# Building the one-hot tiles of a two-layer graph network with scalar_tensor_tensor in place of tensor_scalar

## The chip, the cores and the metric

The kernel runs on one core of a Trainium2 chip. The metric is the device time of one execution in microseconds. Each core has TensorE (matmuls), VectorE, ScalarE, GpSimd and SyncE, which run their own instruction streams and meet at semaphores, and DMA queues. In the profile they are PE (and PEld, its weight loads), DVE, ACT, POOL and SP.

## The reference

The graph has 12,500 nodes of 128 features and 400,000 edges, sorted by their destination. Two layers follow each other:

```python
h = relu(layernorm(x))
# layer 0
edge_in  = concat([h[src], h[dst], edge_attr])          # 128 + 128 + 64
m        = relu(relu(edge_in @ We1 + be1) @ We2 + be2)   # 32, then 128
node_msg = relu(relu(concat([h[dst], m]) @ Wn1 + bn1) @ Wn2 + bn2)
x = x + h + segment_sum(node_msg, dst)
# layer 1
h = relu(layernorm(x))
H   = einsum('ni,rio->rno', h, W)                        # 8 relations
msg = (H[etype, src] + b[etype]) * weight
x = x + relu(segment_sum(msg, dst))
```

## The kernel before

The edges are padded to 782 chunks of 512, each of them four tiles of 128 edges (TC = 4). As the edges are sorted, the destinations of a chunk mostly lie in a window of W = 32 nodes; should some chunk span more, all is repeated in further passes. Here there is one pass. Three stages of node work (layernorm, projections, transposes, storing tables to memory) surround two loops over the chunks, in which nearly all the time goes.

**Layer 0, per chunk.** GpSimd fetches the source nodes' projected rows with four indirect DMAs, one for each tile (`gather`, L517, into `prow`, which lies in the tensor `shared`). SyncE loads the edge attributes, the destinations spread over 96 partitions (`dst_wide`, in `rows_place`) and the 32 table rows of the window. TensorE sums the first hidden layer from all of these (`sum_h1`: L980, L984, and at last L987, which waits for the gathered rows), and then come three more matmul stages with ScalarE and VectorE between them. VectorE builds two one-hot tensors per chunk in `build_hot`: `hot` (L790, in `match_window`: 128 edges by 4 x 32 window places, f32) and `hotT` (L813: 96 rows by 512 edges, bf16), with which TensorE picks the destination's rows. For each chunk VectorE's order is: the relu of `h1` (L818), `build_hot` of the following chunk (L790, L813), the addition of an older chunk to `agg` (L824), the bias of `msg2` (L828).

**Layer 1, per chunk.** GpSimd gathers the source's 128 features in the same way (L517, into `rows`, in `rows_place`). VectorE builds, in `build_hot1`, for two chunks at a time: the offsets in the window (L878, twice), `hot` again (L790) and four tiny `et_w` (L885, 128 x 8: the edge's weight in its relation's column) for each chunk, the key (L888, relation and place in one number), and then for each chunk a series of four `hot_rel` (L900, 128 x 256: the edge's weight at its key, in `shared`). TensorE multiplies the rows by `hot_rel` (L1080), which sorts them by relation and destination, and `hot` by `et_w` (L1082). ScalarE copies the sums, TensorE projects them with the eight relations' weights (L1093, L1095) and VectorE adds the result (L915).

**Order and buffers.** Everything is written out by hand, with no scheduler: each engine's block has its own loop, pipelined over chunks by `pipelined` (layer 0) and `paired` (layer 1). The gathers have four slots (SL = 4); a slot is free once `sum_h1` (layer 0) or `scatter` (layer 1) of its last chunk has run. `hotT` and `hot_rel` have two buffers, `et_w` and `hot` four. A series of `hot_rel` waits for the `scatter` that used its buffer. What GpSimd runs in the two loops is the gathers and nothing else.

Of the kernel before, what the change touches and what calls it, by code (L numbers as in the profile page):

```python
# [23 lines left out]
def gnn_two_layers(nc, x, src_t, dst_t, etype_t, weight_t, dst_c, edge_cols,  # L24
                   we1, be1, we2, be2, wn1, bn1, wn2, bn2, w_rel, b_rel, out):
    f32, bf16, i32, u32 = mybir.dt.float32, mybir.dt.bfloat16, mybir.dt.int32, mybir.dt.uint32
    ALU, ACT, AX = mybir.AluOpType, mybir.ActivationFunctionType, mybir.AxisListType
    ds = bass.ds

    P = 128  # L30
# [4 lines left out]
    TC = 4  # L35
    CH = TC * P
# [4 lines left out]
    W = 32  # L41
# [4 lines left out]
    R = w_rel.shape[0]  # L46
# [19 lines left out]
    with ctx:  # L66
        def sb(name, shape, dt=f32):
            return ctx.enter_context(nc.sbuf_tensor(name, shape, dt))
# [4 lines left out]
        def slot_sems(name, n=SL):  # L73
            return [sem(f"{name}{k}") for k in range(n)]
# [20 lines left out]
        iota_key = sb("iota_key", [P, R, W])  # L95
        row_i = sb("row_i", [3 * W, 1], i32)
        row_f = sb("row_f", [3 * W, 1])
# [4 lines left out]
        et_key = late[:, 0:NCH * TC]  # L102
        w_f = late[:, NCH * TC:]
# [4 lines left out]
        base_c = sb("base_c", [P, NROW])  # L108
# [44 lines left out]
        dst_wide = [rows_place[0:3 * W, s * CH:(s + 1) * CH].bitcast(i32) for s in range(SL)]  # L153
# [3 lines left out]
        RW = R * W  # L157
        hot_rel = [shared[:, k * TC * RW:(k + 1) * TC * RW].rearrange("p (t n) -> p t n", n=RW) for k in range(2)]
        rel_sums = [h[k].rearrange("p j d -> p (j d)")[:, 0:2 * RW].rearrange("p (r c n) -> p r c n", r=R, c=2) for k in range(2)]
        et_w = [sb(f"et_w{s}", [P, TC, R]) for s in range(SL)]  # L160
        w_sums = [sb(f"w_sums{k}", [R, 2, W]) for k in range(2)]
        offset = [sb(f"offset{k}", [P, 2 * TC]) for k in range(2)]
        key = [sb(f"key{k}", [P, 2 * TC]) for k in range(2)]
# [5 lines left out]
        hotT = [sb(f"hotT{s}", [3 * W, CH], bf16) for s in range(2)]  # L169
# [42 lines left out]
        h1_summed, h2_summed, hot_built = slot_sems("h1_summed"), slot_sems("h2_summed"), slot_sems("hot_built")  # L212
# [131 lines left out]
        def hold(eng):  # L344

            eng.nop(nofuse=True)  # L346
# [337 lines left out]
        def _(dve):  # L684
# [103 lines left out]
            def match_window(c):  # L788

                return dve.scalar_tensor_tensor(  # L790
                    out=hot[c.slot][:, :, :], in0=tiled(iota_f[:, 0:W], TC), scalar=base_c[:, ds(c.i, 1)],
                    in1=wide(dst_f[:, ds(c.i * TC, TC)], W), op0=ALU.add, op1=ALU.is_equal)
# [13 lines left out]
            def build_hot(c):  # L806


                s = c.slot
                match_window(c)  # L810
                dve.wait_ge(dst_wide_landed[s], 16 * c.turn + 16)
                hold(dve)
                dve.tensor_scalar(hotT[s % 2][:, :], dst_wide[s], base_c[0:3 * W, ds(c.i, 1)], row_f[:, 0:1],  # L813
                                  ALU.subtract, ALU.is_equal).then_inc(hot_built[s], 1)

            def relu_h1(c):
                dve.wait_ge(h1_summed[c.slot], c.turn + 2)
# [12 lines left out]
            def step(c, before, before2, after):  # L830
                if c:
                    relu_h1(c)
                if after:
                    build_hot(after)
                if before2:
                    add_chunk(before2)
                if before:
                    bias_msg2(before)

            with dve.Fori(0, passes) as m:  # L840
                dve.wait_ge(pass_ready, m + 1)
                hold(dve)
                build_hot(Chunk(m, 0, 0))
                pipelined(m, dve, step)

                set_windows(m + 1, pass_step, pass_ready, 2 * m + 2)
# [25 lines left out]
            def build_hot1(p):  # L872


                k = p.half
                for n, c in enumerate(p.chunks):

                    dve.tensor_scalar(offset[k][:, n * TC:(n + 1) * TC], dst_f[:, ds(c.i * TC, TC)], base_c[:, ds(c.i, 1)],  # L878
                                      -1.0, ALU.subtract, ALU.max).then_inc(offsets_set, 1)
                for n, c in enumerate(p.chunks):  # L880
                    dve.wait_ge(scattered[c.slot], c.turn + 1)
                    match_window(c)
                    for t in range(TC):
                        at = ds(c.i * TC + t, 1)
                        dve.tensor_scalar(et_w[c.slot][:, t, :], iota_key[:, :, 0], et_key[:, at], w_f[:, at],  # L885
                                          ALU.is_equal, ALU.mult)
                dve.wait_ge(offsets_set, 2 * p.n + 2)
                dve.scalar_tensor_tensor(out=key[k][:, :], in0=offset[k][:, :], scalar=float(W), in1=et_key[:, p.tiles],  # L888
                                         op0=ALU.min, op1=ALU.add).then_inc(keys_set, 1)
                dve.wait_ge(keys_set, p.n + 1)  # L890
                for n, c in enumerate(p.chunks):
                    u = c.slot

                    if p.half:
                        dve.wait_ge(scattered[u - 2], p.m * SLOT_USES[u - 2] + p.quad + 2)
                    else:
                        dve.wait_ge(scattered[u + 2], p.m * SLOT_USES[u + 2] + p.quad + 1)
                        dve.wait_ge(scattered[u], c.turn + 1)
                    for t in range(TC):
                        ins = dve.tensor_scalar(hot_rel[u % 2][:, t, :], iota_key[:, :, :].rearrange("p r n -> p (r n)"),  # L900
                                                key[k][:, n * TC + t:n * TC + t + 1], w_f[:, ds(c.i * TC + t, 1)],
                                                ALU.is_equal, ALU.mult)
                    ins.then_inc(hot1_built[u], 1)

            def add_pair(p):
# [12 lines left out]
            def step1(pair, before, after):  # L918
                if after:
                    build_hot1(after)  # L920
                if before:
                    add_pair(before)

            with dve.Fori(0, passes) as m:
                set_windows(m, pass1_step, pass1_ready, 2 * m)
                dve.wait_ge(pass1_ready, m + 1)
                hold(dve)
                build_hot1(Pair(m, 0, 0))
                paired(m, dve, step1)


            for g in range(NG):
                for a, (t0, t1) in enumerate(HALVES):
# [3 lines left out]
                                             op0=ALU.max, op1=ALU.add).then_inc(fin_done, 1)  # L937
# [236 lines left out]
```

## Time and profile before

| | |
|---|---|
| median of 3 runs | 8168.06 us (8164.82 to 8168.57) |
| the profiled execution's own time | 8177.98 us |
| its span, first to last instruction | 8176.1 us |
| mean granted TensorE clock | 0.939 |
| busy: PE, PEld | 6794.7 us (83%), 5258.3 us (64%) |
| busy: POOL, DVE, ACT | 6070.7 (74%), 3968.1 (49%), 2015.0 us (25%) |
| gathers of layer 0 | from 94.9 us on, the last starts at 4140.6 us |
| gathers of layer 1 | from 4212.4 us on, the last starts at 8136.4 us |

In this profile a row of the grouped view has the line, the engine, the operation, what is written and read, the shapes and the count; behind the bar the busy time in us and the mean of one in ns, and behind the second bar the idle time of the engine in front of these instructions with what ended it. "issue" means that the profile shows nothing the engine waited for. A row of the view in time order has the start in us, the length in us, the engine, the line and the count of merged instructions; the engine's idle time before it stands in brackets. The names `shared`, `rows_place` and `late` are large tensors that hold several buffers each: `shared<-p_tab,idx` is layer 0's gather, `rows_place<-h_tab,idx` is layer 1's, and `shared<-iota_key,key,late` is `hot_rel`.

### The profile page before, as it was taken

The numbers are of one execution on the slowest core, as the hardware profiler recorded it, in microseconds if no ns is written. First come the engines' busy times: TensorE is split into PE (matmuls) and PEld (weight loads), VectorE is DVE, ScalarE is ACT, GpSimd is POOL, SyncE is SP. The second block draws the span as 40 slices with busy tenths as digits, with TensorE's granted clock in tenths as the row PEclk, the third lists the DMA queues.
The fourth block names the chain that finished last, engine by engine and source line by source line (L and its number), as shares of the span: only waits on it lengthen the run. The fifth ranks groups of instructions, "written<-read, shape, count | busy, mean of one in ns | idle before, by whom it ended". The sixth has DMA issues, their size and how long they took to land.

```text
span 8176.1 us, 180555 instructions
## 1 busy us (share of the span) xinstructions
PE 6794.7 (83%) x52954; PEld 5258.3 (64%) x52954; DVE 3968.1 (49%) x13460; ACT 2015.0 (25%) x4976; POOL 6070.7 (74%) x6300
## 2 busy tenths in 40 slices
PE   5999999999988999999967787777777777877777
PEld 4666666666666666666656666666666666666665
DVE  5333333333333333333355555555555555555555
ACT  5333333333333333333330000000000000000000
POOL 4777777777777777777757777777777777777776
PEclk7999999999999999999988888988898888888889
DMA  6333333333333333333332222222222222222222
GB/s 130 83 81 81 81 80 80 81 81 81 81 80 81 81 81 81 81 81 80 81 85 53 53 53 53 53 52 53 53 53 53 53 53 53 53 53 53 52 53 75
DMA packets 627942, 566.94 MB, mean 69 GB/s; under 512 B 312595, under 2 KB 502171, under 8 KB 627420
## 3 DMA queue, kind: packets, MB, share of 16 engines
q0 software_dynamic: 200192, 256.65, 15.5%
q1 hardware_dynamic: 427724, 309.99, 13.3%
q8 instruction: 10, 0.16, 0.0%
q14 instruction: 16, 0.13, 0.0%
HBM read 544.42 MB, written 21.68 MB: 69 GB/s over the span
## 4 chain that ended last, share of the span: by engine, by line
POOL 35%; PE 29%; issue 26%; DMA 7%; DVE 1%; ACT 1%; POOLq 1%; SPq 0%; DVEq 0%; ACTq 0%
POOL shared L517 31%; PE bank L1080 19%; DMA rows_place<-h_tab,idx 6%; PE bank L1093 5%; POOL rows_place L517 4%; PE bank L1082 3%; PE bank L1095 1%; ACT h_place L560 1%; PE bank L994 0%; PE bank L1013 0%; POOLq L346 0%; POOLq L512 0%; DMA qr_tab<-late 0%; DVE stats L690 0%; SPq L411 0%
## 5 line engine op out<-in xcount | busy, mean ns | idle before, releaser
L517 POOL DMA_INDIRECT shared<-p_tab,idx x3128 | 3056.4, 977 | 997.1 <-issue 957.4
L517 POOL DMA_INDIRECT rows_place<-h_tab,idx x3128 | 2970.6, 950 | 978.1 <-issue 847.7
L1080 PE MATMUL bank<-shared,rows_place 128*128 128x256 f32 x6256 | 1830.8, 443 | 876.6 <-issue 756.7
L1080 PEld LDWEIGHTS bank<-shared,rows_place 128*128 128x128 f32 x6256 | 1290.7, 217 | 1140.4 <-issue 791.5
L900 DVE TENSOR_SCALAR shared<-iota_key,key,late 128x256 f32<-128x256 f32 x3128 | 1130.9, 423 | 740.6 <-PE bank L1082 603.5
L669 ACT ACTIVATE h_place<-bank 128x256 f32<-128x256 f32 x782 | 300.6, 384 | 3581.6 <-PE bank L1082 3102.2
L994 PE MATMUL bank<-h_sb,w_tile 128*128 128x128 f32 x6256 | 907.6, 288 | 69.5 <-DVE h_sb L818 0.9
L994 PEld LDWEIGHTS bank<-h_sb,w_tile 128*128 128x128 f32 x6256 | 758.5, 191 | 279.6 <-DVE h_sb L818 279.6
L818 DVE TENSOR_SCALAR h_sb<-bank,be_col 128x128 f32<-128x128 f32 x782 | 274.1, 351 | 1339.1 <-PE bank L987 1339.1
L1013 PE MATMUL bank<-wn_half,h_sb 128*128 128x128 f32 x6256 | 890.3, 285 | 0.0
L1093 PE MATMUL bank<-h_place,w_rel_sb 128*128 128x64 f32 x6256 | 859.8, 295 | 0.0
L1093 PEld LDWEIGHTS bank<-h_place,w_rel_sb 128*128 128x128 f32 x6256 | 804.2, 208 | 26.6
L828 DVE TENSOR_TENSOR shared<-bank,bn_rep 128x512 f32<-128x512 f32 x782 | 540.9, 692 | 539.9 <-PE bank L1013 539.9
L1013 PEld LDWEIGHTS bank<-wn_half,h_sb 128*128 128x128 f32 x6256 | 762.3, 192 | 0.0
L620 ACT ACTIVATE shared<-bank,be_col 128x512 f32<-128x512 f32 x782 | 537.4, 687 | 750.7 <-PE bank L994 750.7
L624 ACT ACTIVATE shared<-shared 128x512 f32<-128x512 f32 x782 | 493.2, 631 | 904.3 <-DVE shared L828 822.4
L885 DVE TENSOR_SCALAR et_w<-iota_key,late 128x8 f32<-128x8 f32 x3128 | 694.7, 300 | 0.0
L987 PE MATMUL bank<-ident,shared 128*128 128x128 f32 x1564 | 382.5, 326 | 314.6 <-DMA shared<-p_tab,idx 313.8
L980 PE MATMUL bank<-shared,w_pair 128*128 128x128 f32 x3128 | 557.6, 301 | 51.3 <-DMA shared<-in_edge_cols 51.3
L980 PEld LDWEIGHTS bank<-shared,w_pair 128*128 128x128 f32 x3128 | 408.4, 190 | 291.4 <-issue 240.0
L915 DVE TENSOR_TENSOR agg<-agg,bank 128x32 f32 x782 | 147.6, 189 | 815.3 <-PE bank L1095 498.4
L790 DVE SCALAR_TENSOR_TENSOR hot<-iota_f,base_c,dst_f 128x128 f32<-128x128 f32 x1564 | 536.1, 343 | 1.2 <-issue 1.2
(93 smaller groups left out, 5328.6 us busy)
## 6 DMA issues: line engine op xcount, KB each, us to landing
rows_place<-in_dst_c SPq DMA_DIRECT2D x782, 192.0 KB
shared<-in_edge_cols SPq DMA_DIRECT2D x782, 128.0 KB
shared<-p_tab,idx POOLq DMA_INDIRECT x3128
rows_place<-h_tab,idx POOLq DMA_INDIRECT x3128
qr_w<-qr_tab SPq DMA_DIRECT2D x782, 18.0 KB
qr_tab<-late SPq DMA_DIRECT2D x21, 336.0 KB, 5.7
res<-in_x SPq DMA_DIRECT2D x14, 448.0 KB, 6.9
idx<-in_src_t SPq DMA_DIRECT2D x392, 8.0 KB
```

The source lines that it names most:

```text
L517: pool.indirect_dma_start(out=rows_of[s][:, t, :], out_offset=None, in_=table, in_offset=bass.IndirectOffsetOnAxis(ap=idx[k][:, s * TC + t ...
L620: act.activation(msg1_sb[:, :], ps_msg1[:, :], ACT.Relu, bias=be2_col[:, 0:1]).then_inc(msg1_done, 1)
L624: act.activation(msg2_sb[:, :], msg2_sb[:, :], ACT.Relu).then_inc(msg2_done, 1)
L790: return dve.scalar_tensor_tensor(out=hot[c.slot][:, :, :], in0=tiled(iota_f[:, 0:W], TC), scalar=base_c[:, ds(c.i, 1)], in1=wide(dst_f[:, ...
L828: dve.tensor_tensor(msg2_sb[:, :], ps_msg2[:, :], bn2_rep[:, :], ALU.add).then_inc(msg2_biased, 1)
L885: dve.tensor_scalar(et_w[c.slot][:, t, :], iota_key[:, :, 0], et_key[:, at], w_f[:, at], ALU.is_equal, ALU.mult)
L900: ins = dve.tensor_scalar(hot_rel[u % 2][:, t, :], iota_key[:, :, :].rearrange("p r n -> p (r n)"), key[k][:, n * TC + t:n * TC + t + 1], ...
L980: pe.matmul(ps_h1[:, 0:P], w1_pair[:, q, :], ea[s][:, q * P:(q + 1) * P], start=(q == 0), stop=False)
L994: ins = pe.matmul(ps_msg1[:, t * P:(t + 1) * P], w2_tile[:, t, :], h1_sb[:, :], start=True, stop=True)
L1013: ins = pe.matmul(ps_msg2[:, t * P:(t + 1) * P], h2_sb[:, b * P:(b + 1) * P], wn2_half[:, a, :], start=True, stop=True)
L1080: pe.matmul(bank[s][:, 0:RW], rows[s][:, t, :], hot_rel[s % 2][:, t, :], start=(t == 0), stop=(t == TC - 1))
L1093: pe.matmul(there, w_rel_sb[:, r, :], rel_sums[p.half][:, r, :, :].rearrange("p c n -> p (c n)"), start=(r == 0), stop=False)
```

## The change

Three instructions are written with another operation. `tensor_scalar` takes one tensor and two scalars, here both a column with one value for each partition, and does two operations with them. `scalar_tensor_tensor` takes a tensor, one scalar and a second tensor. The second column becomes this second tensor, by repeating it along the row (`broadcast_to`, no copy in memory). The computed values, the shapes, the types and the waits are the same, and so is the order of the instructions on each engine: on VectorE 782 `hotT`, 3128 `et_w` and 3128 `hot_rel` are SCALAR_TENSOR_TENSOR in place of TENSOR_SCALAR, and on the other engines nothing differs.

```diff
@@ build_hot (layer 0) @@
                 dve.wait_ge(dst_wide_landed[s], 16 * c.turn + 16)
                 hold(dve)
-                dve.tensor_scalar(hotT[s % 2][:, :], dst_wide[s], base_c[0:3 * W, ds(c.i, 1)], row_f[:, 0:1],
-                                  ALU.subtract, ALU.is_equal).then_inc(hot_built[s], 1)
+                dve.scalar_tensor_tensor(out=hotT[s % 2][:, :], in0=dst_wide[s], scalar=base_c[0:3 * W, ds(c.i, 1)],
+                                         in1=row_f[:, 0:1].broadcast_to([3 * W, CH]), op0=ALU.subtract, op1=ALU.is_equal)\
+                   .then_inc(hot_built[s], 1)
@@ build_hot1 (layer 1) @@
                     for t in range(TC):
                         at = ds(c.i * TC + t, 1)
-                        dve.tensor_scalar(et_w[c.slot][:, t, :], iota_key[:, :, 0], et_key[:, at], w_f[:, at],
-                                          ALU.is_equal, ALU.mult)
+                        dve.scalar_tensor_tensor(out=et_w[c.slot][:, t, :], in0=iota_key[:, :, 0], scalar=et_key[:, at],
+                                                 in1=w_f[:, at].broadcast_to([P, R]), op0=ALU.is_equal, op1=ALU.mult)
...
                     for t in range(TC):
-                        ins = dve.tensor_scalar(hot_rel[u % 2][:, t, :], iota_key[:, :, :].rearrange("p r n -> p (r n)"),
-                                                key[k][:, n * TC + t:n * TC + t + 1], w_f[:, ds(c.i * TC + t, 1)],
-                                                ALU.is_equal, ALU.mult)
+                        ins = dve.scalar_tensor_tensor(
+                            out=hot_rel[u % 2][:, t, :], in0=iota_key[:, :, :].rearrange("p r n -> p (r n)"),
+                            scalar=key[k][:, n * TC + t:n * TC + t + 1],
+                            in1=w_f[:, ds(c.i * TC + t, 1)].broadcast_to([P, RW]), op0=ALU.is_equal, op1=ALU.mult)
                     ins.then_inc(hot1_built[u], 1)
```

## Rows read from the trace of the kernel before

**Rows 1.** The page's busy totals: busy us (share of the span) and instructions.
```profile
PE 6794.7 (83%) x52954; PEld 5258.3 (64%) x52954; DVE 3968.1 (49%) x13460; ACT 2015.0 (25%) x4976; POOL 6070.7 (74%) x6300
```

**Rows 2.** The page's costliest groups: the gathers, hot_rel and the bias of msg2.
```profile
L517 POOL DMA_INDIRECT shared<-p_tab,idx x3128 | 3056.4, 977 | 997.1 <-issue 957.4
L517 POOL DMA_INDIRECT rows_place<-h_tab,idx x3128 | 2970.6, 950 | 978.1 <-issue 847.7
L900 DVE TENSOR_SCALAR shared<-iota_key,key,late 128x256 f32<-128x256 f32 x3128 | 1130.9, 423 | 740.6 <-PE bank L1082 603.5
...
L828 DVE TENSOR_TENSOR shared<-bank,bn_rep 128x512 f32<-128x512 f32 x782 | 540.9, 692 | 539.9 <-PE bank L1013 539.9
```

**Rows 3.** The view of L517: duration ns min/median/max, first and last start us.
```profile
L517 POOL DMA_INDIRECT shared<-p_tab,idx x3128: 940/945/1218, 94.9 to 4140.6; - x196
L517 POOL DMA_INDIRECT rows_place<-h_tab,idx x3128: 940/945/1133, 4212.4 to 8136.4; - x196
```

**Rows 4.** Waits: us in total, times, longest us.
```profile
PE bank L987 <- DMA shared<-p_tab,idx: 313.8, 752, 1.6
...
POOL shared L517 <- DMA idx<-in_src_t: 37.3, 1, 37.3
```

**Rows 5.** In order of time, layer 0, one chunk: VectorE and GpSimd.
```profile
1999.52 0.54 DVE L813 TENSOR_SCALAR hotT<-rows_place,base_c,row_f 96x512 bf16<-96x512 int32 x1
...
1999.80 1.07 POOL L517 DMA_INDIRECT shared<-p_tab,idx  x1 [0.30 <-issue]
...
2000.83 0.19 DVE L824 TENSOR_TENSOR agg<-agg,bank 128x32 f32 x1 [0.78 <-PE bank L1029]
2001.18 0.94 POOL L517 DMA_INDIRECT shared<-p_tab,idx  x1 [0.30 <-issue]
...
2002.43 0.95 POOL L517 DMA_INDIRECT shared<-p_tab,idx  x1 [0.30 <-issue]
...
2003.68 0.94 POOL L517 DMA_INDIRECT shared<-p_tab,idx  x1 [0.31 <-issue]
...
2004.60 0.54 DVE L813 TENSOR_SCALAR hotT<-rows_place,base_c,row_f 96x512 bf16<-96x512 int32 x1
...
2004.93 1.03 POOL L517 DMA_INDIRECT shared<-p_tab,idx  x1 [0.30 <-issue]
```

**Rows 6.** In order of time, layer 0: three meetings of hotT and a gather.
```profile
2158.82 0.57 DVE L813 TENSOR_SCALAR hotT<-rows_place,base_c,row_f 96x512 bf16<-96x512 int32 x1
2158.93 0.94 POOL L517 DMA_INDIRECT shared<-p_tab,idx  x1 [0.30 <-issue]
...
2565.23 0.54 DVE L813 TENSOR_SCALAR hotT<-rows_place,base_c,row_f 96x512 bf16<-96x512 int32 x1
2565.36 1.22 POOL L517 DMA_INDIRECT shared<-p_tab,idx  x1 [0.30 <-issue]
...
2862.27 0.54 DVE L813 TENSOR_SCALAR hotT<-rows_place,base_c,row_f 96x512 bf16<-96x512 int32 x1
2862.69 0.94 POOL L517 DMA_INDIRECT shared<-p_tab,idx  x1 [0.30 <-issue]
```

**Rows 7.** In order of time, layer 1: hot (L790) and a gather, twice.
```profile
4543.45 0.34 DVE L790 SCALAR_TENSOR_TENSOR hot<-iota_f,base_c,dst_f 128x128 f32<-128x128 f32 x1
4543.54 1.07 POOL L517 DMA_INDIRECT rows_place<-h_tab,idx  x1 [0.30 <-PE bank L1082]
...
7513.15 0.34 DVE L790 SCALAR_TENSOR_TENSOR hot<-iota_f,base_c,dst_f 128x128 f32<-128x128 f32 x1
7513.17 1.13 POOL L517 DMA_INDIRECT rows_place<-h_tab,idx  x1 [0.30 <-PE bank L1082]
```

**Rows 8.** Views of single lines, VectorE: duration ns min/median/max, first and last start.
```profile
L813 DVE TENSOR_SCALAR hotT<-rows_place,base_c,row_f x782: 533/536/712, 142.6 to 4139.8; 96x512 bf16<-96x512 int32 x196
L900 DVE TENSOR_SCALAR shared<-iota_key,key,late x3128: 394/406/653, 4214.7 to 8132.1; 128x256 f32<-128x256 f32 x196
L885 DVE TENSOR_SCALAR et_w<-iota_key,late x3128: 274/283/547, 4212.5 to 8128.5; 128x8 f32<-128x8 f32 x196
L790 DVE SCALAR_TENSOR_TENSOR hot<-iota_f,base_c,dst_f x1564: 335/343/353, 135.3 to 8127.7; 128x128 f32<-128x128 f32 x196
L888 DVE SCALAR_TENSOR_TENSOR key<-offset,late x391: 149/156/233, 4214.4 to 8128.7; 128x8 f32<-128x8 f32 x196
```

**Rows 9.** In order of time, layer 1: a series of hot_rel and a gather.
```profile
4254.99 1.38 DVE L900 TENSOR_SCALAR shared<-iota_key,key,late 128x256 f32<-128x256 f32 x4 [0.22 <-DVE key L888]
...
4255.46 1.08 POOL L517 DMA_INDIRECT rows_place<-h_tab,idx  x1 [0.30 <-issue]
```

## The prediction

> **What bounds the kernel now.** Read first the busy totals [rows 1]: TensorE is busy for 83% of the span, GpSimd for 74%, VectorE for 49%. That looks like a kernel bound by TensorE, but the GpSimd share leaves out the short pause before each gather. In the costliest groups [rows 2] the 3128 gathers of layer 0 take 3056.4 us, with 997.1 us of idle time before them, together 4053.5 us; by their first and last start and their length [rows 3] they stand from 94.9 to 4141.5 us, 4046.6 us. So no time in layer 0 is without a gather or its pause (one wait of 37.3 us, for the indices, comes early on [rows 4]). The same sum in layer 1 is 2970.6 + 978.1 = 3948.7 us, against 4212.4 to 8137.3 us = 3925 us (the first idle stretch lies before it). The median gather is 0.945 us and the pause 0.30 [rows 3, 5]: GpSimd starts one every 1.249 us and never waits for a slot. TensorE waits for it instead: in 752 of 782 chunks of layer 0 the matmul of L987 waits for the gathered rows [rows 4]. Whatever lengthens a gather lengthens the kernel by as much, and what VectorE takes longer for costs nothing by itself.
>
> What lengthens gathers now? The mean of layer 0 is 977 ns against a usual 0.944 us: 3128 x 33 ns = 103 us in all, 132 ns per chunk of four. Layer 1 has 950 ns: 3128 x 6 = 18 us. In time order [rows 5] three gathers of four take 0.94 or 0.95 us, and the fourth, which starts while hotT (L813) runs, takes 1.03 to 1.07. The extra time follows a formula. In [rows 6] hotT starts at 2565.23 and ends at 2565.77; the gather started at 2565.36 and took 1.22, 0.28 too much. The end of hotT less 0.28 is 2565.49, 0.13 us after the gather's start. At 2004.60 + 0.54 = 2005.14 and a gather from 2004.93 with 0.09 extra it is 0.12. So a gather wants something 0.125 us after its start that hotT holds to its end. Two edges confirm it: where hotT ends at 2862.81 and the gather started at 2862.69, it is not held up; where hotT starts at 2158.82 and the gather at 2158.93, the moment (2159.06) falls 0.24 us after hotT's start, the gather gets through at 0.94 and hotT takes 0.57 in place of 0.54. At 0.26 us after the start (the 2565 case) hotT was ahead. A two-scalar TENSOR_SCALAR holds that something from about 0.25 us after its start to its end.
>
> **Does a SCALAR_TENSOR_TENSOR hold it?** This decides the case. The trace has one with two SBUF inputs and a column as scalar: hot, L790. In layer 0 it is over before the gather's moment, but in layer 1 it meets it 22 times, and each of the 22 gathers is held up. In [rows 7] L790 runs from 4543.45 to 4543.79, the gather from 4543.54 takes 1.07, 0.13 too much: 4543.66, 0.12 after the start, as before. At 7513.15 it starts 0.02 before the gather and still holds it up by 0.19. So it holds from at most 0.15 us after its start: a wider share of the instruction than now. Its second input is a broadcast column too (dst_f, repeated along each window).
>
> A rule of the Trainium skill speaks against me in part. Its page "SBUF — State Buffer", section "Who interferes with whom", says that a VectorE instruction with two SBUF inputs contends only with a GpSimd instruction that reads SBUF, and infers that such an operation does not stall a software DMA, whose descriptors need the write interface. By the inference the change would free the gathers, and the sum would be the rival "freed" below. The L790 rows contradict it for this indirect gather.
>
> **The change part by part.** No instruction moves, and no wait or DMA is added; three kinds of instruction get other durations and another hold.
>
> hotT, 782 times in layer 0. Now 536 ns for 512 elements [rows 8]. L900 takes 406 for 256 and L885 283 for 8: 123 ns for 248 elements, about 0.5 ns each, so TENSOR_SCALAR from SBUF moves two elements per 1.04 ns. SCALAR_TENSOR_TENSOR has two rows: L888 with 8 elements 156 ns (no column scalar), L790 with 128 elements and a column 343. I take 1.04 ns per element, as L828 bears out (512 elements from PSUM, 692 [rows 2]), and 343 - 133 = 210 ns fixed: 210 + 533 = 743 ns, 207 more than now. Ends: 692 as L828, and 275 (L885's fixed part) + 533 = 808. The phase of hotT to the gather stays: L987 waits for a gather, L818, L790 and L813 follow at fixed distances, and the held gather is the third one after that, paced by GpSimd. So the end of hotT comes 207 ns later relative to it, and the held gather takes 207 ns more: 782 x 0.98 x 207 = 159 us, and 3 us for the 2% that slip by now (the 2158.82 case of [rows 6]) and will be caught: 162 us. Ends 120 (156 ns) and 211 us (272 ns). L824 comes 1.31 us after hotT's start [rows 5], so the longer hotT delays nothing on VectorE.
>
> hot_rel, 3128 times in layer 1: 210 + 267 = 477 ns for 406. It holds for 477 - 150 = 327 ns, now for some 140. VectorE's instructions in a series overlap by about 80 ns, and GpSimd gets in between (the 4255.46 gather of [rows 9] loses 0.13 us, not the rest of the series). A gather's moment comes every 1249 ns; a hold of length H meets it with chance H/1249 and costs H/2: 327 x 327 / 2498 = 43 ns, x 3128 = 134 us. The same formula gives the present hold 7.8 ns, 25 us, where the trace has 18: it is of the right size, with phases that are not evenly spread. Ends: 0, if the series settles between the moments, and about one full hold per series, 0.33 us x 782 = 255 us, since a gather held up pushes the next moment out of the series.
>
> et_w, 3128 times: 210 + 8 = 218 ns for 283. The 65 ns gained (203 us of VectorE) are off the path. The hold of 68 ns costs 68 x 68 / 2498 = 2 ns, 6 us; ends 0 and 20. The present 18 us go. Layer 1: 134 + 6 - 18 = 122 us, ends -18 and 257.
>
> VectorE in layer 1: 4 x (71 - 65) = 24 ns more per chunk of 5.0 us, with waits of 603.5 us for TensorE in front of L900 [rows 2]; it stays uncritical.
>
> Sum: 162 + 122 = 284 us. Against the profiled execution (8177.98 us, 1.9 outside the span of 8176.1) that is 8462; that execution stands 10 us over the median of the runs, 8168.06, to which I add: 8452. All low ends give 8270, all high ends 8636.
>
> **Rivals.**
> *Series in step, 8312 us.* Layer 1's series locks its phase between the moments, so only hotT's 162 us come and the 18 go. For it: many L900 now end just before a gather's moment. Against: L900 starts at two differently released places per pair, key and TensorE.
> *Freed, 8047 us (faster).* If an input that is one repeated column holds nothing after its first element, or if only write traffic counts, all stalls go: 8168 - 103 - 18. It decides at the first hotT that runs over a gather's 0.125 us point: that gather then takes 0.944. For it: the repeated column differs from L790's, which changes every 32 elements. Against: 22 of 22 in layer 1.
> *Nothing, 8168.* The new form is run as the old one, two elements at a time, with the same hold. Against: L790's 343 ns for 128 elements.
> *Shut out, 9190 us.* The holds of successive SCALAR_TENSOR_TENSOR join, so a gather waits for the end of a series of 3 x 400 + 477 = 1.68 us: 1.68 x 1.68 / 2.498 = 1.13 us x 782 = 884, with hotT's 162, less 18 (rounded). Against: VectorE's next instruction has to wait for its own turn; L790 followed by L885 let the gather in at L790's end.
>
> **Numbers.** Forecast 0.72, in step 0.12, freed 0.08, nothing 0.03, shut out 0.05. The likeliest is 8452 us. A range of 8290 to 8590 takes in the "in step" case and most of the bounds of the three durations and phases. A measurement of this kernel tells about 0.2% (16 us) from no change: faster 0.08, same 0.03, slower 0.89.
>
> **What would show it.** The changed profile should have hotT at about 743 ns, hot_rel 477, et_w 218; the gathers of layer 0 at a mean near 977 + 52 = 1029 ns, one in four at 1.2 to 1.4 us, in layer 1 near 950 + 39 = 989; TensorE's wait for gathered rows in front of L987's matmul larger, and DVE busy up by 160 us in layer 0. Layer 0's share is right if hotT's end less the gather's extra time is again 0.125 us after the gather's start. I am wrong if gathers over hotT take 0.944 us (freed), or if hotT ends near 0.54 (nothing).

## The result and the profile after

The changed kernel takes 8405.65 us (median of 4 runs, 8396.84 to 8406.13), the kernel before 8168.32 us beside it (8164.82 to 8168.99): 237 us more, ratio 1.0289 with a 95% interval of 1.0271 to 1.0307. The forecast was 8452 us in a range of 8290 to 8590.

The page of the changed kernel, busy totals and the two gathers (columns as in [rows 1, 2]):

```profile
PE 6812.9 (81%) x52954; PEld 5269.9 (63%) x52954; DVE 4115.1 (49%) x13460; ACT 2012.7 (24%) x4976; POOL 6296.5 (75%) x6300
...
L517 POOL DMA_INDIRECT shared<-p_tab,idx x3128 | 3199.2, 1023 | 994.5 <-issue 957.6
L517 POOL DMA_INDIRECT rows_place<-h_tab,idx x3128 | 3053.7, 976 | 978.2 <-issue 879.8
```

Against [rows 2] the gathers of layer 0 take 142.8 us more and those of layer 1 83.1 us more, with the same pauses. That is 226 of the 228 us by which the profiled span grew (8404.3 from 8176.1; by the medians it is 237, as the profiled execution of the kernel before stood 10 us over its median). TensorE works as long as before and only waits longer for gathered rows, 454.6 us in place of the 313.8 of [rows 4]:

```profile
PE bank L989 <- DMA shared<-p_tab,idx: 454.6, 760, 1.7
```

The three changed instructions, view of single lines (minimum/median/maximum in ns), to be read against [rows 8]:

```profile
L813 DVE SCALAR_TENSOR_TENSOR hotT<-rows_place,base_c,row_f x782: 736/741/791, 142.0 to 4279.6; 96x512 bf16<-96x512 int32 x196
L901 DVE SCALAR_TENSOR_TENSOR shared<-iota_key,key,late x3128: 470/480/555, 4354.4 to 8355.7; 128x256 f32<-128x256 f32 x196
L886 DVE SCALAR_TENSOR_TENSOR et_w<-iota_key,late x3128: 211/220/289, 4352.7 to 8351.2; 128x8 f32<-128x8 f32 x196
```

In order of time, one chunk of layer 0 in the changed kernel, which answers to [rows 5]:

```profile
2000.63 0.74 DVE L813 SCALAR_TENSOR_TENSOR hotT<-rows_place,base_c,row_f 96x512 bf16<-96x512 int32 x1
...
2001.01 1.18 POOL L517 DMA_INDIRECT shared<-p_tab,idx  x1 [0.30 <-issue]
...
2001.95 0.19 DVE L825 TENSOR_TENSOR agg<-agg,bank 128x32 f32 x1 [0.57 <-PE bank L1031]
2002.50 0.94 POOL L517 DMA_INDIRECT shared<-p_tab,idx  x1 [0.30 <-issue]
```

hotT ends at 2001.37, the gather took 0.24 us too long, and 2001.37 - 0.24 = 2001.13, 0.12 us after its start: the formula of the prediction. Of the 766 gathers that hotT held up in this trace, 98 in 100 give a difference between 0.120 and 0.130 us. The addition to agg still follows after a pause (0.57 us in place of 0.78), so the longer hotT delays nothing else.

### The profile page after: what moved, and what is told of

The parts are those of the page before. It is cut to its first block, busy times and chain, and to the rows that moved or that the text cites. A ratio compares the mean times of both kernels' runs of the same rounds, so it can differ in the third digit from the quotient of the medians.

```text
span 8404.3 us, 180555 instructions
## 1 busy us (share of the span) xinstructions
PE 6812.9 (81%) x52954; PEld 5269.9 (63%) x52954; DVE 4115.1 (49%) x13460; ACT 2012.7 (24%) x4976; POOL 6296.5 (75%) x6300
## 4 chain that ended last, share of the span: by engine, by line
POOL 35%; PE 30%; issue 27%; DMA 6%; DVE 1%; ACT 1%; POOLq 1%; SPq 0%; DVEq 0%; ACTq 0%
POOL shared L517 32%; PE bank L1082 20%; DMA rows_place<-h_tab,idx 5%; PE bank L1095 5%; POOL rows_place L517 3%; PE bank L1084 3%; PE bank L1097 1%; ACT h_place L560 1%; PE bank L996 0%; POOLq L346 0%; POOLq L512 0%; PE bank L1015 0%; DMA qr_tab<-late 0%; DVE stats L690 0%; SPq L411 0%
## 5 line engine op out<-in xcount | busy, mean ns | idle before, releaser
L517 POOL DMA_INDIRECT shared<-p_tab,idx x3128 | 3199.2, 1023 | 994.5 <-issue 957.6
L517 POOL DMA_INDIRECT rows_place<-h_tab,idx x3128 | 3053.7, 976 | 978.2 <-issue 879.8
L1082 PE MATMUL bank<-shared,rows_place 128*128 128x256 f32 x6256 | 1889.5, 455 | 947.5 <-issue 801.8
L1082 PEld LDWEIGHTS bank<-shared,rows_place 128*128 128x128 f32 x6256 | 1338.0, 225 | 1223.7 <-issue 838.4
L901 DVE SCALAR_TENSOR_TENSOR shared<-iota_key,key,late 128x256 f32<-128x256 f32 x3128 | 1308.6, 480 | 953.4 <-PE bank L1084 870.5
L1095 PE MATMUL bank<-h_place,w_rel_sb 128*128 128x64 f32 x6256 | 833.2, 290 | 0.0
L1095 PEld LDWEIGHTS bank<-h_place,w_rel_sb 128*128 128x128 f32 x6256 | 778.3, 202 | 25.1
L989 PE MATMUL bank<-ident,shared 128*128 128x128 f32 x1564 | 382.5, 326 | 454.7 <-DMA shared<-p_tab,idx 454.6
L989 PEld LDWEIGHTS bank<-ident,shared 128*128 128x128 f32 x1564 | 232.9, 188 | 560.5 <-DMA shared<-p_tab,idx 559.0
L813 DVE SCALAR_TENSOR_TENSOR hotT<-rows_place,base_c,row_f 96x512 bf16<-96x512 int32 x782 | 580.3, 742 | 7.3 <-DMA rows_place<-in_dst_c 7.3
L790 DVE SCALAR_TENSOR_TENSOR hot<-iota_f,base_c,dst_f 128x128 f32<-128x128 f32 x1564 | 537.9, 344 | 1.2 <-issue 1.2
```

The source lines that it names most:

```text
L517: pool.indirect_dma_start(out=rows_of[s][:, t, :], out_offset=None, in_=table, in_offset=bass.IndirectOffsetOnAxis(ap=idx[k][:, s * TC + t ...
L790: return dve.scalar_tensor_tensor(out=hot[c.slot][:, :, :], in0=tiled(iota_f[:, 0:W], TC), scalar=base_c[:, ds(c.i, 1)], in1=wide(dst_f[:, ...
L813: dve.scalar_tensor_tensor(out=hotT[s % 2][:, :], in0=dst_wide[s], scalar=base_c[0:3 * W, ds(c.i, 1)], in1=row_f[:, 0:1].broadcast_to([3 * ...
L901: ins = dve.scalar_tensor_tensor(out=hot_rel[u % 2][:, t, :], in0=iota_key[:, :, :].rearrange("p r n -> p (r n)"), scalar=key[k][:, n * TC ...
L989: pe.matmul(ps_h1[:, 0:P], prow[s][:, :, :].rearrange("p t o -> p (t o)"), ident[:, :], start=False, stop=True)\
L1082: pe.matmul(bank[s][:, 0:RW], rows[s][:, t, :], hot_rel[s % 2][:, t, :], start=(t == 0), stop=(t == TC - 1))
```

## The experiments

In this section a gather is "held up" when it took over 0.01 us longer than its usual 0.944 us. Its "point" is the moment 0.125 us after its start. Sums of the extra time, and what VectorE was running at the gather's 0.125 us point, are counted over all the rows of a trace.

**hotT alone.** The diff is the first hunk of the change.

> Only hotT is a SCALAR_TENSOR_TENSOR; layer 1 is as before. Theory (a gather reads at 0.125 us after its start and waits there for the end of a VectorE instruction that holds what both need): layer 0 as in the changed kernel, its gathers 143 us above before (3199.2 against 3056.4), layer 1's gathers at 2971 us: 8168 + 141 = 8309 us. Rival, that the two layers' costs aren't separate (hot_rel's part is caused by something hotT leaves behind, or the reverse): another split than 141 and 83.

Measured: 8331.97 us against 8167.01, ratio 1.0194 (1.0174 to 1.0215), 165 us more and 23 us over the 8309 expected.

```profile
L517 POOL DMA_INDIRECT shared<-p_tab,idx x3128 | 3201.4, 1023 | 996.3 <-issue 958.3
L517 POOL DMA_INDIRECT rows_place<-h_tab,idx x3128 | 2981.3, 953 | 978.7 <-issue 840.9
```

Layer 0 gives 145 us, as in the changed kernel. Layer 1, in which nothing was changed, lost 11 us too. So differences of this size in layer 1 between two builds say nothing on the change.

**hot_rel alone.** The diff is the last hunk of the change.

> Only hot_rel is a SCALAR_TENSOR_TENSOR (477 ns, holding for some 270). Theory: layer 1's gathers 3054 us in place of 2971, a little less if et_w had a part in it, layer 0 unchanged: 8168 + 80 = 8248 us, between 8225 and 8265 as the phases of the series fall. Rival, that et_w's new form makes most of layer 1's cost: below 8190.

Measured: 8288.89 us, ratio 1.0150 (1.0133 to 1.0166), 122 us more, outside what was expected.

```profile
L517 POOL DMA_INDIRECT rows_place<-h_tab,idx x3128 | 3099.3, 991 | 978.7 <-issue 886.9
L517 POOL DMA_INDIRECT shared<-p_tab,idx x3128 | 3046.0, 974 | 995.8 <-issue 959.0
```

Layer 1's gathers take 129 us more than before, and in the changed kernel only 83. hot_rel holds up gathers for 117 us here and for 100 there. Most of the rest is hot (L790), which no one changed: it runs over the point of 260 gathers, some 195 of them held up for 26 us together, where in the kernel before it was 22 and 3 us, and in the changed kernel it is 1.7 us.

In layer 1 this kernel and the changed one differ in et_w alone, so et_w's new form gives back some 46 us there. Its own hold has no part in that. With the longer series VectorE comes to hot at another phase, and what runs just ahead of hot counts as well. Here a gather's point (5447.70) lies 0.13 us after hot's start, right behind an et_w in its old form, and the gather waits for hot's end:

```profile
5446.78 0.87 DVE L885 TENSOR_SCALAR et_w<-iota_key,late 128x8 f32<-128x8 f32 x4
5447.57 0.34 DVE L790 SCALAR_TENSOR_TENSOR hot<-iota_f,base_c,dst_f 128x128 f32<-128x128 f32 x1
5447.58 1.15 POOL L517 DMA_INDIRECT rows_place<-h_tab,idx  x1 [0.30 <-PE bank L1083]
```

Behind an old et_w read from SBUF hot held up each of the 169 gathers whose point it ran over, and it did so in every trace at this clock (322 of 322 with this one, 94 of them with the point less than 0.16 us after hot's start). Behind the new et_w or the offsets, 6 of 269 gathers with so early a point were held up. Why the instruction ahead matters was not tested.

**One input from SBUF.** The repeated column and iota_key are copied into the free PSUM bank 6 and read there.

```diff
-                dve.tensor_scalar(hotT[s % 2][:, :], dst_wide[s], base_c[0:3 * W, ds(c.i, 1)], row_f[:, 0:1],
-                                  ALU.subtract, ALU.is_equal).then_inc(hot_built[s], 1)
+                dve.scalar_tensor_tensor(out=hotT[s % 2][:, :], in0=dst_wide[s], scalar=base_c[0:3 * W, ds(c.i, 1)],
+                                         in1=bank[6][0:3 * W, 0:1].broadcast_to([3 * W, CH]), ...
-   et_w, hot_rel: tensor_scalar(..., iota_key...)
+   et_w, hot_rel: tensor_scalar(..., bank[6][:, 0:RW] ...)   # copied there before the layer 1 loop
```

> hotT is a SCALAR_TENSOR_TENSOR whose repeated column is read from PSUM; hot_rel and et_w are TENSOR_SCALAR whose tensor (iota_key) is read from PSUM. Each has one input tensor from SBUF at most, and as long a run as the changed kernel's (hotT about 745 ns or a few tens more, hot_rel about 480). Theory, that the hold comes with a second stream from SBUF: no gather is held up, both layers' gathers at 0.944 us mean, 8168 - 103 - 18 = 8047 us. Rival, that any VectorE instruction of this length which runs over the gather's 0.125 us point holds it up: 8400 us, as the changed kernel. Rival, that it is the operation SCALAR_TENSOR_TENSOR in any form: layer 0 + 140, layer 1 - 18, 8290 us.

Measured: 8056.86 us, ratio 0.9867 (0.9850 to 0.9883): faster than both kernels. Groups and single lines of its profile, and a meeting in order of time:

```profile
L518 POOL DMA_INDIRECT shared<-p_tab,idx x3128 | 2962.6, 947 | 995.1 <-issue 958.7 <-DMA idx<-in_src_t 34.5 <-PE bank L993 1.8
L518 POOL DMA_INDIRECT rows_place<-h_tab,idx x3128 | 2958.6, 946 | 978.8 <-issue 833.9 <-PE bank L1088 144.8
```
```profile
L816 DVE SCALAR_TENSOR_TENSOR hotT<-rows_place,base_c,bank x782: 732/737/744, 142.5 to 4045.9; 96x512 bf16<-96x512 int32 x196
L906 DVE TENSOR_SCALAR shared<-bank,key,late x3128: 529/535/546, 4121.0 to 8029.1; 128x256 f32<-128x256 f32 x196
```
```profile
3002.53 0.74 DVE L816 SCALAR_TENSOR_TENSOR hotT<-rows_place,base_c,bank 96x512 bf16<-96x512 int32 x1
3002.89 0.94 POOL L518 DMA_INDIRECT shared<-p_tab,idx  x1 [0.30 <-issue]
```

hotT is the same operation and as long as in the changed kernel (737 and 741 ns), and it runs over the 0.125 us point of 766 gathers, of which 2 were held up, by 0.013 us on average. hot_rel, 535 ns and longer than in either kernel, runs over that of 1057, 4 of them held up. In the same trace hot, which still has two inputs from SBUF, held up four gathers, by 0.05 to 0.16 us. Both rivals fall: neither length nor the operation holds a gather up. For SCALAR_TENSOR_TENSOR it is the second input from SBUF. For the old form two things went at once: its tensor no longer comes from SBUF, and it no longer moves two elements at a time (535 ns for 256 elements and 276 for 8 are 1.04 ns for each). The run doesn't part them.

**Another place for hotT.** In layer 0's step, `build_hot(after)` goes behind `add_chunk(before2)`.

```diff
-                if after:
-                    build_hot(after)
                 if before2:
                     add_chunk(before2)
+                if after:
+                    build_hot(after)
                 if before:
                     bias_msg2(before)
```

> hotT alone is a SCALAR_TENSOR_TENSOR (as in hotT_alone), and build_hot stands after the addition to agg (L824) in place of ahead of it, so hotT starts some 0.13 us after a gather's start, holds from about 0.34 to 0.87 us after it and is over before the next gather's 0.125 us point. Theory (only the moment at 0.125 us counts for a SCALAR_TENSOR_TENSOR): gathers of layer 0 at 944 ns mean, 8168 - 103 = 8065 us. Rival, that it is the length of hotT or TensorE's and VectorE's chain that costs the time: 8309 us as hotT_alone, or more. Rival, that a SCALAR_TENSOR_TENSOR holds up later parts of a gather too, as the present form does: extra time of 0.3 us per chunk, 8300 us.

Measured: 8102.12 us, ratio 0.9920 (0.9904 to 0.9937).

```profile
303.51 0.35 DVE L790 SCALAR_TENSOR_TENSOR hot<-iota_f,base_c,dst_f 128x128 f32<-128x128 f32 x1
303.63 1.04 POOL L517 DMA_INDIRECT shared<-p_tab,idx  x1 [0.30 <-issue]
303.77 0.74 DVE L813 SCALAR_TENSOR_TENSOR hotT<-rows_place,base_c,row_f 96x512 bf16<-96x512 int32 x1
...
3002.86 0.94 POOL L517 DMA_INDIRECT shared<-p_tab,idx  x1 [0.30 <-issue]
3002.87 0.35 DVE L790 SCALAR_TENSOR_TENSOR hot<-iota_f,base_c,dst_f 128x128 f32<-128x128 f32 x1
3003.14 0.74 DVE L813 SCALAR_TENSOR_TENSOR hotT<-rows_place,base_c,row_f 96x512 bf16<-96x512 int32 x1
```

The same long hotT, 0.28 us after the gather's start, leaves it at 0.94 us: of a gather's course only its point counts. What is left of layer 0's extra time (23 us) is mostly hot, which now stands where hotT stood: at 303.51 it ends at 303.86, 0.10 us after the point, and the gather has 0.10 too much. 198 gathers lost 18 us to it. With 5 us from layer 1 that makes most of the 37 us to the 8065 expected; some 9 are not accounted for.

**The old form in the same place** (the diff above on the kernel before). It ran twice, since the first chip was another case (below).

> The kernel before with build_hot behind the addition to agg, as in mid_hot_stt, but hotT in its old form. Theory (only a hold over the gather's 0.125 us point counts, and here hotT's isn't over it in either form): what is left in layer 0 are hot's stalls (18 us in mid_hot_stt), 8168 - 103 + 20 = 8085 us, the same as mid_hot_stt (8102) within 20 us. Rival, that the old form also holds up later parts of a gather (its descriptor writes): over 8130 us.

> The same kernel as mid_hot_ts, for the same reason. Where the kernel before takes some 8168 us: theory (neither form costs where its hold isn't over the gather's 0.125 us point) 8085 us, within 20 us of mid_hot_stt (8102); rival, that the old form also holds up a gather's later parts, over 8130 us.

Measured the second time: 8105.93 us, ratio 0.9926 (0.9909 to 0.9942), equal to mid_hot_stt. hotT in the old form held up gathers for 0.5 us in all of layer 0, hot for 25 us. Off the point the form of hotT makes no difference to the gathers. It does to hotT itself: all 16 hotT in the old form that started 0.43 to 0.60 us after a gather ended late (610 to 762 ns in place of 536), each as if it had waited until 0.655 us after the gather's start. In the new form none of the 19 that started there did (744 ns at most).

**hotT in halves.** On the changed kernel:

```diff
-                dve.scalar_tensor_tensor(out=hotT[s % 2][:, :], in0=dst_wide[s], ...)
+                for half in range(2):
+                    cols = slice(half * CH // 2, (half + 1) * CH // 2)
+                    ins = dve.scalar_tensor_tensor(out=hotT[s % 2][:, cols], in0=dst_wide[s][:, cols], ...)
```

> The changed kernel with hotT written by two SCALAR_TENSOR_TENSOR of 256 columns in place of one of 512: some 480 ns each, 0.88 us together with their overlap of 0.08, so VectorE works longer for hotT than the changed kernel's 0.742. Theory (a hold from 0.2 us after the start to the end of each instruction, GpSimd gets in between): the first half holds to 0.48 us after hotT's start, and the gather's moment lies at 0.42 on average; from the changed kernel's starts hotT's stalls would sum to 47 us in place of 243: 8406 - 196 = 8210 us, 8190 to 8250 with the phase's uncertainty. Rival, that VectorE's time (or the chain through it) is what costs: 8406 + 782 x 0.13 = 8508 us. Rival, that holds in a row join: the same 8508.

> The same kernel as hotT_in_halves, because there TensorE was granted 0.81 of its clock, the kernel before took 10429 us and GpSimd waited for TensorE. Where the kernel before takes some 8168 us: theory (a hold per instruction, from 0.2 us after its start to its end) 8210 us, 8190 to 8250; rival, that VectorE's time costs or that holds in a row join, 8508 us. Should the kernel before be slow again, nothing is told apart.

Measured the second time: 8206.48 us (8202.2 to 8210.67), 199 us under the changed kernel, with 8210 expected.

```profile
3001.25 0.87 DVE L815 SCALAR_TENSOR_TENSOR hotT<-rows_place,base_c,row_f 96x256 bf16<-96x256 int32 x2
3001.53 1.02 POOL L517 DMA_INDIRECT shared<-p_tab,idx  x1 [0.30 <-issue]
```

The first half ends at 3001.72 (0.47 us each), 0.07 us after the point, and the gather loses 0.08 though VectorE goes on to 3002.12. 592 gathers lost 47 us to hotT, in place of 244. More work on VectorE made the kernel faster, since the hold over the point is shorter.

**hot_rel in halves.** On the changed kernel, in the same manner.

> The changed kernel with each hot_rel written by two SCALAR_TENSOR_TENSOR of 128 columns, 344 ns each, so a series takes some 2.2 us of VectorE in place of 1.67. Theory, by the formula hold x hold / (2 x 1249): hold 0.14 us, 6256 x 7.8 ns = 49 us in place of 100: 8406 - 51 = 8355 us, between 8320 and 8400 as the phases fall. Rival, that VectorE's time costs: 8406 + 782 x 0.5 = 8800 us, or part of it.

> The same kernel as hot_rel_in_halves, for the same reason. Where the kernel before takes some 8168 us: theory (hold squared over 2 x 1249 ns) 8355 us, 8320 to 8400; rival, that VectorE's longer series costs, 8500 us or more.

Measured the second time: 8418.28 us, ratio to before 1.0308 (1.0291 to 1.0325). This missed: 8355 was expected, and it came out 13 us above the changed kernel. hot_rel held up gathers for 112 us where the formula gave 49, and hot for 12. Two things are in the rows. Of the 485 gathers whose point lay in a half that had more than 0.185 us to run, one was held up, of the others all: the hold is 0.185 us of 0.347, not 0.14. And 152 gathers waited for two halves:

```profile
4418.21 1.26 POOL L517 DMA_INDIRECT rows_place<-h_tab,idx  x1 [0.30 <-issue]
4418.31 0.35 DVE L903 SCALAR_TENSOR_TENSOR shared<-iota_key,key,late 128x128 f32<-128x128 f32 x1
```

The half before this one ends at 4418.40, 0.06 us after the point at 4418.34; the 0.32 us that the gather took too long lead to the end of the next, 4418.66. This is the rival "shut out" for one step. The place in the series decides it: of the 152, 147 had their point over the seventh half of eight, with the last one behind it. There all 147 gathers with a point 0.04 to 0.08 us ahead of the half's end waited for the eighth too, and over the sixth half 2 of 134. A series of four whole hot_rel doesn't show it: in the changed kernel all 43 gathers with such a point over the third went on at its end. Why stays open. VectorE's longer series as such cost nothing: the pauses in front of layer 1's gathers are 978.2 us, as before.

**et_w alone, and a chip with a lower clock.** The diff is the second hunk of the change.

> Only et_w is a SCALAR_TENSOR_TENSOR (221 ns for 300). Theory: its own hold is too short to count (0 us in the changed kernel), its shorter time only moves what follows to another phase: 8168 us, within 20 us of it. Rival, that et_w's new form by itself frees part of layer 1 (hot_rel_alone lost 46 us more in layer 1 than the changed kernel did): 8120 us.

> The same kernel as et_w_alone, where the kernel before takes some 8168 us. Theory: et_w's own hold costs nothing, its shorter time (221 ns for 300, four in a row) only moves hot and the series of hot_rel to other phases of the gathers: within 20 us of 8168. In hot_rel_alone hot's (L790's) holds cost 26 us and in the changed kernel 2, so hot may cost less here too, by its 3 us at most. Rival, that et_w's new form is worth 46 us in layer 1 by itself (the difference between hot_rel_alone and the changed kernel there): 8120 us.

Measured: ratio 1.0016 (0.9995 to 1.0037) and 0.9994 (0.9976 to 1.0012), no difference. But beside them the kernel before took 10429 and 10414 us. TensorE was granted 0.81 of its clock there, a mean of stretches at 2.4 and at 1.2 GHz, and the gathers no longer followed each other at their own pace. In the first run of hotT_in_halves these waits stand in front of them (us in total, times, longest us):

```profile
POOL shared L517 <- remote: 904.6, 516, 2.6
POOL rows_place L517 <- remote: 763.4, 304, 3.9
POOL shared L517 <- PE bank L993: 625.3, 226, 8.6
```

"remote" is a wait whose end the profile puts down to no engine. By the program a gather waits for its indices or for TensorE to free its slot, so it was most likely TensorE too. All idle time in front of the gathers is 4058 us there and 1975 us in the kernel before.

There the gathers aren't the bound all the time, and the ratios of hotT_in_halves (0.9881), hot_rel_in_halves (1.0818) and mid_hot_ts (0.9945) on that chip say nothing on the question. et_w alone was thus never measured where the gathers are the bound. Its own hold is read from the changed kernel's trace: it ran over 345 points, and the extra time there sums to 0.0 us. What it does through hot is read from hot_rel_alone (above), beside the new hot_rel. The kernel before can't give back the rival's 46 us, as layer 1's gathers lose 18 us there in all.

## Why the prediction was right, and where its sizes were off

The bound was read rightly: the gathers' extra time makes 226 of the 228 us, and where it went away (one input from SBUF) the kernel came to 8057 us, near the 8047 of "freed".

The deciding step, that a SCALAR_TENSOR_TENSOR with two SBUF inputs holds up an indirect gather, was right. It stood on 22 meetings of hot in layer 1, and 766 meetings of hotT in the changed kernel confirm it. (The prediction has hot always over in time in layer 0. In the kernel before it ran over 5 points there, and all 5 gathers were held up.) That "freed" was wrong for a column repeated along the row is shown: such an input holds to the end. A second tensor that isn't repeated does the same, as a subtraction of two tensors in SBUF shows in the changed kernel, ahead of the chunks:

```profile
115.66 1.56 DVE L768 TENSOR_TENSOR agg<-agg,late 128x1344 f32<-128x1344 f32 x1 [3.34 <-ACT late L590]
115.95 2.09 POOL L517 DMA_INDIRECT shared<-p_tab,idx  x1 [0.30 <-issue]
```

It ends at 117.22, and less the gather's 1.15 us too much this is 116.07, again 0.12 us after its start. The inference on the page "SBUF — State Buffer" of the Trainium skill ("Who interferes with whom"), that two SBUF inputs do not stall a software DMA, does not hold for the start of these gathers. Its rule behind that, that GpSimd's reads meet the second input, agrees with the point being a single one near the gather's start; no run shows which data is read there.

The durations 743, 477 and 218 ns came out as 741, 480 and 220.

hotT's term was 162 us and measured 143. The step that failed is the fixed phase. hotT starts 0.026 us earlier against the gather that it holds up (0.298 in place of 0.272 us ahead of it, mean of 680 chunks), as L987 finds the gathered rows sooner after the last gather's start (2.394 in place of 2.422 us). So the held gather lost 182 ns more (318 on average, 136 before), not 207. Why the rows come sooner was not tested; with longer chunks less data moves per us (78 in place of 81 GB/s).

Layer 1's term was 122 us and measured 83. The 134 us of hot_rel came out as 100, mainly since the hold was sized too long. That it begins 0.15 us after the start was read from a single row, the hot at 7513.15 of [rows 7]. That is right for hot behind an old et_w and did not carry over to hot_rel: in the changed kernel the gathers were all held up whose point lay in a hot_rel that ended up to 0.42 us after the gather's start, and of 227 where it ended 0.45 us or more after it one was. A hold of 0.295 us gives 0.295 x 0.295 / 2.498 x 3128 = 109 us. The 18 us that were to go went, but for hot's 1.7.

Read by single changes, the term that was most off is et_w's. hot_rel alone made layer 1's gathers 129 us longer, where its two terms give 134 - 18 = 116. et_w was put at 6 us, its shorter time at nothing, as off the path; its own hold cost nothing, and in company with hot_rel its new form gave some 46 us back, 24 of them at hot and 17 at hot_rel. That is a comparison of two builds, with 11 us to be allowed for.

"In step" did not come about: 675 of the 925 hot_rel that ran over a point held the gather up.

## What to carry to other kernels

Where GpSimd's indirect gathers are the bound, the form of a VectorE instruction counts by whether it reads two inputs from SBUF (or one, two elements at a time), and by whether it then runs over the moment at which a gather starts; its own time may count for nothing. Turning a scalar column into a broadcast tensor made the hold longer; reading one of the operands from PSUM took it away for both forms. Before a change, lay the ends of VectorE's instructions against the starts of the stretched gathers: a constant difference names the culprit and gives a first price. Changing one instruction also moves the others against the gathers, and in layer 1 that was worth 46 us beside the 129 of hot_rel alone.

## What the runs showed of the hardware

- The gather (0.944 us) has one point, 0.125 us after its start, where a SCALAR_TENSOR_TENSOR or TENSOR_TENSOR with two SBUF inputs, or a TENSOR_SCALAR in the old form, holds it up until that instruction ends. In mid_hot_stt hotT ran over most of the rest of a gather and left it at 0.944 us.
- The hold begins some 0.2 us after the instruction's own start (hotT, hot_rel in the new form) or 0.25 us (old form). For hot right behind an old et_w it begins by 0.08 us.
- An instruction that comes later waits instead: hot took up to 0.422 us in place of 0.343 in mid_hot_stt where it started 0.06 to 0.1 us ahead of a gather and did not hold it up. The old hotT also waited for something late in a gather when it started 0.43 to 0.60 us after the gather (712 ns in [rows 8], up to 762 in mid_hot_ts_again), which the new form never did there.
- In hot_rel_in_halves_again 152 gathers waited for two SCALAR_TENSOR_TENSOR in a row, nearly all at the last two of a series.
- The same kernel took 8168 us on a chip that granted 0.94 of TensorE's clock and 10429 us on one that granted 0.81.
